# A fused graph layer and two-expert feed-forward: memory of their own for twelve of sixteen slots of unit rows, and rows asked for five units ahead

## The chip, the cores and the metric

One core of one Trainium2 chip runs the kernel. The metric is the device time of one execution in microseconds (us), the median of several runs; lower is better.

## The reference

The input `x` is 128 graphs x 128 nodes x 128 features, so 16,384 tokens. A graph layer is followed by a mixture of eight experts, of which each token uses two.

```python
def reference(x, adj, ...):
    x = x + gnn(layernorm(x), adj, adj, ...)      # two adjacency products per graph, sigmoid gates, relu
    x = x + ffn(layernorm(x), Wg, bg, W1, b1, W2, b2)
    return x

def ffn(xf, ...):                                 # xf: 16384 x 128
    gate_logits = xf @ Wg + bg                    # 8 experts
    top_w, top_i = top_k(gate_logits, 2); top_w = softmax(top_w)
    w_dense = sum(one_hot(top_i, 8) * top_w[..., None], axis=1)
    for e in range(8):                            # W1[e]: 128 x 512, W2[e]: 512 x 128
        out += w_dense[:, e:e+1] * (gelu(xf @ W1[e] + b1[e]) @ W2[e] + b2[e])
    return out
```

How many tokens an expert gets depends on the data; the kernel finds it out as it runs.

## The kernel before, in words

**First phase: 16 chunks.** A chunk is 8 graphs (1,024 tokens). For each chunk the engines work out the graph layer, the second layer norm and the two experts of each token, and write one row of 260 floats per token into `row`, a ring of five chunk slots in the on-chip memory: 128 normed values, 128 values of the running sum, two weights, the row's place in pass two, and the token's number. GpSimd (POOL) then scatters the rows of the chunk into a table `rows` in device memory, eight indirect DMAs of 128 rows per chunk (line 591), sorted by the token's lower expert, in the order of chunks within an expert.

**Second phase: 140 units.** A unit is 256 rows of one expert. Pass one (units 0 to 69) goes through the rows by lower expert, pass two (units 70 to 139) by higher expert; in each pass a few units are blank because experts do not fill their last unit. Per unit:
- SyncE (SP) loads its 256 rows (260 KB) from `rows` into one of `GR` = 16 slots (`rows_in`, line 474), and its biases.
- TensorE (PE) turns the rows (`unit_turned`, line 1377), does layer one (`layer1`, 12 matmuls, lines 1391 to 1393), layer two of the unit before (`layer2`, 12 matmuls, lines 1403 to 1408) and turns the result back (`unit_back`, line 1419). Its program is in order: `layer1(k)`, `unit_back(k-2)`, `layer2(k-1)`, `unit_turned(k+3)`.
- ScalarE does gelu, VectorE splits the hidden values into a high and a low part, weights the result and adds it to the row (`sum_up`).
- POOL scatters the unit's rows: in pass one back into `rows`, to their place in pass two (line 637); in pass two to the output (line 634).

**Weights.** Three slots hold the weights of a layer, so when the expert changes, the next three units each load both layers anew (512 KB a layer, line 490, `layer_in`); otherwise SP just counts the slot's semaphore up. A slot may be overwritten only after the unit three before has read it: layer one's load of unit k+2 waits for the first layer of unit k-1.

**SP's order.** At step k: layer one's weights and the biases of unit k+2, layer two's weights of unit k+1, then the rows of unit k+`AHEAD`, with `AHEAD` = 4. Before step 0 it reads some entries of a unit table that VectorE has worked out, and issues the first `AHEAD` row copies. Everything that SP waits for holds back all that stands behind it.

**Where rows may be loaded, and when.** All sixteen slots of unit rows lie in chunk slots 1 to 4 of the ring `row`: units 0 to 3 in slot 1, which chunk 11 held, units 4 to 7 in slot 2 (chunk 12), 8 to 11 in slot 3 (chunk 13), 12 to 15 in slot 4 (chunk 14). A slot is free once its chunk has been scattered. Also, a unit's rows must have landed in `rows`. `wait_landed` (line 509) sees to both. The first 12 chunks (`PART`) are waited for at the outset. The table gives each of units 0 to 7 a number `least`: 1 if all of its rows come from the first 12 chunks, 5 if it must wait for chunks 12 to 15 as well; POOL counts `s_land` up as each late chunk lands (line 619). Unit 4 waits for `s_land` 2, so that chunk 12 has left slot 2; unit 8 waits for 5, that is for all. In pass two, units 70 to 81 wait for a number of landed units of pass one from the table (`needs`), and unit 82 for all.

Of the kernel before, what the change touches and what calls it, by code (L numbers as in the profile page):

```python
# [8 lines left out]
I32 = mybir.dt.int32  # L9
U32 = mybir.dt.uint32  # L10
ALU = mybir.AluOpType
# [3 lines left out]
P = 128  # L15
G = 8
# [4 lines left out]
BLK = TILE // P  # L21


ROW = 2 * P + 4
W_AT, NEXT_AT, TOKEN_AT = 2 * P, 2 * P + 2, 2 * P + 3
# [3 lines left out]
BIG = float(1 << 23)  # L29
# [24 lines left out]
def wait_turn(eng, sem, each, turn, more):  # L54

    value = turn.group * (each * turn.unroll) + (each * turn.step + more)
    if not isinstance(value, int) or value > 0:
        eng.wait_ge(sem, value)


def wait_slot(eng, sems, each, turn, more):

    ring = len(sems)
    s = turn.slot(ring)
    wait_turn(eng, sems[s], each, Turn(turn.group, (turn.step - s) // ring, turn.unroll // ring, 0), more)
# [20 lines left out]
def program(nc, x, x_turned, adj, edges, gate_weights, gate_biases, Wg, bg, W1, W2, biases, out):  # L86
# [11 lines left out]
    NROWS = 2 * (E - 1) * TOKENS + 2 * TILE  # L98
    UA, UT = 4, 16

    WR, BR, GR, AHEAD = 3, 8, 16, 4

    EARLY = [2 * AHEAD, 3 * AHEAD]

    IN, BACK = 3, 2

# [2 lines left out]
    PART = CHUNKS - 4  # L109

    RING = 5
# [15 lines left out]
    def bank_of_outputs(k):  # L127
        return 5 + 2 * (k + BACK) % 3

    def bank_of_rows(k):  # L130
        return 5 + (2 * (k - IN) + 1) % 3

    w_dram = nc.dram_tensor("w_split", (E, 2, P, 2 * H), F32).ap()
    rows = nc.dram_tensor("rows", (NROWS, ROW), F32).ap()
    out_rows = out.rearrange("b n d -> (b n) d")

    with ExitStack() as ctx:
        def sb(name, shape, dt=F32):
            return ctx.enter_context(nc.sbuf_tensor(name, list(shape), dt))

        def sem(name):
            return ctx.enter_context(nc.semaphore(name))
# [3 lines left out]
        ident = sb("ident", [P, P])  # L146
# [33 lines left out]
        row = sb("row", [P, RING, G, ROW])  # L180
# [55 lines left out]
        skip = sb("skip", [P, UNITS, BLK])  # L236
# [9 lines left out]
        b_t = sb("b_t", [P, BR, FC + 1])  # L246


        assert GR * BLK == 4 * G and (PART - 1) % RING == 1 and GR == 4 * AHEAD
        got = row[:, 1:5].rearrange("p r (s j) k -> p (r s) j k", j=BLK)  # L250
        got_i = got.bitcast(I32)
        to_row = sb("to_row", [P, GR, BLK], I32)
        in_hi = sb("in_hi", [P, IN, TILE], F32R)
        in_lo = sb("in_lo", [P, IN, TILE], F32R)
# [37 lines left out]
        def ps_o(t):  # L292
            return bank[:, bank_of_outputs(t.index), 0:TILE].rearrange("p (j m) -> p j m", j=BLK)

        def ps_x(t):
            return bank[:, bank_of_rows(t.index), 0:TILE]
# [41 lines left out]
        s_land = sem("late_chunks_landed")  # L338
# [38 lines left out]
        def _(sp):  # L377
# [77 lines left out]
            def entries(column, first, n, most, least=0):  # L455
                _, values = nc.values_load_multi_w_load_instructions(
                    table[column:column + 1, bass.ds(first, n)], engines=[mybir.EngineType.SP], min_val=least, max_val=most,
                    skip_runtime_bounds_check_because="VectorE makes the table's entries from counts that lie in these bounds")
                return values
# [9 lines left out]
            def rows_in(t, both):  # L469
                if t.real:  # L470
                    at = sp.snap(both >> 4, min_val=0, max_val=BLANK + 1)
                    g = t.slot(GR)
                    wait_slot(sp, s_out, 16 * BLK, t, 0)
                    sp.dma_start(got[:, g].rearrange("p j k -> p (j k)"),
                                 rows[bass.ds(at, TILE)].rearrange("(p j) k -> p (j k)", j=BLK)).then_inc(s_got[g], 16)

            def layer_in(t, code_, layer):
# [26 lines left out]
            early = entries(PASSES, 0, AHEAD, MOST)  # L504
            least = entries(2 * PASSES + 1, 0, EARLY[0], CHUNKS - PART + 1, 1)
            for i in range(4):
                sp.wait_ge(s_row[i], 16 * G * PART // 4)

            def wait_landed(k, needs):

                if k < EARLY[0]:
                    if k == AHEAD:
                        sp.wait_ge(s_land, 2)
                    sp.wait_ge(s_land, least[k] & 7)
                elif k == EARLY[0]:
                    sp.wait_ge(s_land, CHUNKS - PART + 1)
                if NU <= k < NU + EARLY[1]:
                    sp.wait_ge(s_landed, needs[k - NU] & 127)
                elif k == NU + EARLY[1]:
                    sp.wait_ge(s_landed, NU + 1)  # L520

            for k in range(AHEAD):
                wait_landed(k, None)
                rows_in(unit(k), early[k])
# [6 lines left out]
            for first in range(0, UNITS, UT):  # L531
                if first > 0:
                    now = codes(first, UT + 2)
                if first <= NU - AHEAD < first + UT:
                    early = entries(PASSES + 1, 0, AHEAD, MOST)
                if first < NU + EARLY[1] - AHEAD and first + UT > NU - AHEAD:
                    needs = entries(2 * PASSES, 0, EARLY[1], NU + 1, 1)
                for k in range(first, min(first + UT, UNITS)):
                    i = k - first
                    if k + 2 < UNITS:  # L540
                        layer_in(unit(k + 2), now[i + 2], 0)
                        biases_in(unit(k + 2), now[i + 2])
                    if k + 1 < UNITS:
                        layer_in(unit(k + 1), now[i + 1], 1)
                    if k + AHEAD < UNITS:
                        wait_landed(k + AHEAD, needs)
                        rows_in(unit(k + AHEAD), early[k + AHEAD - NU] if 0 <= k + AHEAD - NU < AHEAD else now[i])
# [4 lines left out]
        def _(pool):  # L552
# [68 lines left out]
            def landed(t):  # L621
                wait_slot(pool, s_out, 16 * BLK, t, 16 * BLK)
                pool.sem_inc(s_landed, 1)

            def scatter(t):
                second = t.index >= NU
                if 0 <= t.index - 3 < NU:
                    landed(t.back(3))
                wait_turn(pool, s_done, 1, t, 1)
                g = t.slot(GR)  # L630
                for j in range(BLK):
                    at = bass.IndirectOffsetOnAxis(ap=to_row[:, g, j:j + 1], axis=0)
                    if second:
                        pool.indirect_dma_start(out=out_rows, out_offset=at, in_=got[:, g, j, P:2 * P], in_offset=None,  # L634
                                                bounds_check=TOKENS - 1, oob_is_err=False).then_inc(s_out[g], 16)
                    else:
                        pool.indirect_dma_start(out=rows, out_offset=at, in_=got[:, g, j, :], in_offset=None,  # L637
                                                bounds_check=NROWS - 1, oob_is_err=False).then_inc(s_out[g], 16)

            for k in range(UNITS):  # L640
                scatter(unit(k))
# [136 lines left out]
        def _(dve):  # L778
# [382 lines left out]
            for i in range(2):  # L1161
# [3 lines left out]
            first, rows_of, seg, lim, at, start = (unit_at_[:, i] for i in range(6))  # L1165
# [7 lines left out]
                                         in1=start_f[:].unsqueeze(1).to_broadcast([P, 2, PASSES]), op0=ALU.mult, op1=ALU.add))  # L1173
# [14 lines left out]
                                         op0=ALU.add, op1=ALU.is_gt))  # L1188
# [21 lines left out]
            for j in range(BLK):  # L1210
                own(dve.scalar_tensor_tensor(out=skips[:, j], in0=ps_ends[:, 0, :, 0:NU], scalar=slot_f[:, j:j + 1],
                                             in1=skips[:, j], op0=ALU.is_gt, op1=ALU.max))
# [17 lines left out]
            def sum_up(t):  # L1230
                g, second = t.slot(GR), int(t.index >= NU)
                wait_turn(dve, s_o, 1, t, 1)
                at = TOKEN_AT if second else NEXT_AT

                dve.scalar_tensor_tensor(out=to_row[:, g, :], in0=skip[:, t.index, :], scalar=BIG, in1=got_i[:, g, :, at],
                                         op0=ALU.mult, op1=ALU.max)
                for j in range(BLK):
                    w = got[:, g, j, W_AT + second:W_AT + second + 1]
                    last = dve.scalar_tensor_tensor(out=got[:, g, j, P:2 * P], in0=ps_o(t)[:, j, :], scalar=w,  # L1239
                                                    in1=got[:, g, j, P:2 * P], op0=ALU.mult, op1=ALU.add)  # L1240
                last.then_inc(s_done, 1)

            units = range(UNITS)
# [9 lines left out]
            for k in units[-BACK - 1:]:  # L1253
                sum_up(unit(k))

        @block.tensor
        def _(pe):
# [108 lines left out]
            for i in range(2):  # L1366
                for k in range(PASSES):
                    last = pe.matmul(ps_ends[:, i, k], ends_rep[:, i, k], ident[:], start=True, stop=True)
            last.then_inc(s_ends_ps, 1)

            def unit_turned(t):
                g = t.slot(GR)
                wait_slot(pe, s_got, 16, t, 16)

                wait_turn(pe, s_done, 1, t, -IN - BACK)
                for j in range(BLK):
                    last = pe.transpose(ps_x(t)[:, j * P:(j + 1) * P], got[:, g, j, 0:P], ident[:])  # L1377
                last.then_inc(s_xt, 1)

            def layer1(t):  # L1380
# [102 lines left out]
```

## Time and profile before

| | |
|---|---|
| runs | 740.89, 740.40, 737.95 us; median 740.4 |
| profiled execution, span from the first to the last instruction | 738.4 us (its time beyond the span is not given) |
| PE busy | 657.4 us, 89% of the span |
| VectorE (DVE) | 617.8 us, 84% |
| ScalarE (ACT) | 525.4 us, 71% |
| POOL | 500.8 us, 68% |
| bytes moved by DMA | 148.47 MB, 201 GB/s over the span |
| mean granted TensorE clock | 0.950 |

In the profile the first phase takes up the first 240 us or so and the units the rest. A wait is put down to the instruction that ended it. The granted clock is a share of full speed (2.4 GHz). The ends of matmuls are modelled, so that PE can be shown busy over a short wait; the weight loads (PEld), which run beside the matmuls, show such waits as well.

### The profile page before, as it was taken

The page shows a single profiled execution, that of the slowest core. Times are in us where ns is not written, and L with a number is a line of the kernel's source. Part 1 is how long each engine was busy: PE and PEld are TensorE (multiplying, and loading weights), DVE is VectorE, ACT ScalarE, POOL GpSimd, SP SyncE. Part 2 cuts the span into 40 slices and gives each one's busy share as a digit, 9 for nine tenths or more (in the row PEclk, how much of TensorE's full clock was granted, in tenths as well). Part 3 has the DMA queues.
Part 4 walks back from the last instruction along what each step waited for, and adds up shares of the span by engine and source line. Part 5 has one row for each costly group of instructions (what it writes and reads, how often), then busy time and mean ns, then how long its engine had stood idle before and what let it go on. Part 6 is the DMA issues. An engine that isn't in the chain of part 4 may idle for free.

```text
span 738.4 us, 17622 instructions
## 1 busy us (share of the span) xinstructions
PE 657.4 (89%) x4878; PEld 598.6 (81%) x4878; DVE 617.8 (84%) x2056; ACT 525.4 (71%) x1470; POOL 500.8 (68%) x469
## 2 busy tenths in 40 slices
PE   6879888998873979999998999999999999999990
PEld 4646666666562879888998999998999999999990
DVE  4899999999997658777887888887888888888881
ACT  5689999999961646666666767766767767767760
POOL 2652767767767857675776776777777777777773
PEclk9999999899955889999999999999999999999996
DMA  8999994547223567599569655499764444444310
GB/s 296 348 369 275 352 324 152 195 147 313 95 87 109 184 175 249 196 339 320 166 213 356 189 163 156 138 325 378 226 168 120 131 122 121 131 124 119 102 40 29
DMA packets 82040, 148.47 MB, mean 201 GB/s; under 512 B 32247, under 2 KB 36352, under 8 KB 81936
## 3 DMA queue, kind: packets, MB, share of 16 engines
q1 hardware_dynamic: 62576, 100.37, 44.3%
q0 software_dynamic: 18496, 46.70, 17.5%
q8 instruction: 41, 0.67, 0.4%
q14 instruction: 63, 0.52, 0.2%
q10 hardware_dynamic: 864, 0.21, 0.1%
HBM read 92.37 MB, written 57.23 MB: 203 GB/s over the span
## 4 chain that ended last, share of the span: by engine, by line
PE 58%; ACT 18%; DMA 8%; DVE 6%; issue 4%; POOL 3%; SPq 1%; POOLq 0%; ACTq 0%; DVEq 0%
PE bank L1391 8%; PE bank L1403 8%; PE bank L1392 8%; PE bank L1393 8%; PE bank L1408 8%; PE bank L1404 8%; DMA row<-rows 7%; ACT hs L687 5%; ACT row L696 5%; PE bank L1377 4%; ACT t_loop L678 4%; PE bank L1419 4%; ACT t_in L671 3%; POOL rows L591 2%; PE bank L1277 1%
## 5 line engine op out<-in xcount | busy, mean ns | idle before, releaser
L756 ACT ACTIVATE act_f<-bank,b_t 128x256 f32<-128x256 f32 x560 | 220.0, 476 | 7.8 <-PE bank L1393 1.6
L637 POOL DMA_INDIRECT rows<-row,to_row x140 | 167.2, 1194 | 74.0 <-issue 51.9
L634 POOL DMA_INDIRECT out_dram<-row,to_row x140 | 168.0, 1200 | 60.2 <-issue 56.4
L591 POOL DMA_INDIRECT rows<-row,slot_low x128 | 136.4, 1066 | 64.5 <-issue 34.8
L1228 DVE TENSOR_TENSOR act_lo<-act_f,act_hi 128x1024 fp32r<-128x1024 f32 x140 | 171.6, 1225 | 4.8
L746 ACT ACTIVATE in_hi<-bank 128x256 fp32r<-128x256 f32 x140 | 53.9, 385 | 154.9 <-PE bank L1377 154.9
L1223 DVE CAST act_hi<-act_f 128x1024 fp32r<-128x1024 f32 x140 | 97.8, 699 | 69.8 <-ACT act_f L756 69.6
L1391 PE MATMUL bank<-in_hi,w_t 128*128 128x256 f32 x376 | 113.5, 302 | 0.0
L1392 PE MATMUL bank<-in_lo,w_t 128*128 128x256 f32 x376 | 105.5, 281 | 0.0
L1393 PE MATMUL bank<-in_hi,w_t 128*128 128x256 f32 x376 | 105.5, 281 | 0.0
L1403 PE MATMUL bank<-act_hi,w_t 128*128 128x256 f32 x376 | 101.2, 303 | 0.2 <-DVE act_hi L1223 0.2
L1404 PE MATMUL bank<-act_hi,w_t 128*128 128x256 f32 x376 | 92.8, 281 | 0.0
L1239 DVE SCALAR_TENSOR_TENSOR row<-bank,row 128x128 f32<-128x128 f32 x280 | 83.7, 338 | 0.0
L1403 PEld LDWEIGHTS bank<-act_hi,w_t 128*128 128x128 f32 x376 | 71.4, 190 | 0.4 <-issue 0.4
L1392 PEld LDWEIGHTS bank<-in_lo,w_t 128*128 128x128 f32 x376 | 71.5, 190 | 0.0
L1404 PEld LDWEIGHTS bank<-act_hi,w_t 128*128 128x128 f32 x376 | 71.5, 190 | 0.0
L1391 PEld LDWEIGHTS bank<-in_hi,w_t 128*128 128x128 f32 x376 | 71.3, 190 | 0.0
L1393 PEld LDWEIGHTS bank<-in_hi,w_t 128*128 128x128 f32 x376 | 71.1, 189 | 0.0
L1377 PE MATMUL bank<-ident,row 128*128 128x128 f32 x280 | 55.8, 281 | 17.2 <-DMA row<-rows 16.6
L763 ACT ACTIVATE y_t<-bank,b_t 128x256 f32<-128x256 f32 x140 | 66.0, 471 | 3.9 <-PE bank L1408 3.9
L1218 DVE TENSOR_TENSOR in_lo<-bank,in_hi 128x256 fp32r<-128x256 f32 x140 | 57.2, 409 | 8.7 <-ACT in_hi L746 8.7
L687 ACT ACTIVATE hs<-xs,shift,rstd 128x128 f32<-128x128 f32 x128 | 53.6, 655 | 8.5 <-DVE t_sum L894 6.7
(225 smaller groups left out, 1658.9 us busy)
## 6 DMA issues: line engine op xcount, KB each, us to landing
row<-rows SPq DMA_DIRECT2D x140, 260.0 KB, 3.7
w_t<-w_split SPq DMA_DIRECT2D x38, 512.0 KB, 6.7
w_up<-w_split SPq DMA_DIRECT2D x18, 512.0 KB, 7.0
xs<-in_x_dram SPq DMA_DIRECT2D x16, 512.0 KB, 5.0
x_t<-in_x_turned_dram SPq DMA_DIRECT2D x16, 512.0 KB, 6.2
rows<-ends_rep SPq DMA_DIRECT2D x15, 260.0 KB, 7.8
b_t<-in_biases_dram SPq DMA_DIRECT2D x140, 2.5 KB
rows<-row,to_row POOLq DMA_INDIRECT x140, 3.7
```

The source lines that it names most:

```text
L591: pool.indirect_dma_start(out=rows, out_offset=bass.IndirectOffsetOnAxis(ap=slot_low[:, r, b:b + 1], axis=0), in_=row[:, r, b, :], in_offs ...
L634: pool.indirect_dma_start(out=out_rows, out_offset=at, in_=got[:, g, j, P:2 * P], in_offset=None, bounds_check=TOKENS - 1, oob_is_err=Fals ...
L637: pool.indirect_dma_start(out=rows, out_offset=at, in_=got[:, g, j, :], in_offset=None, bounds_check=NROWS - 1, oob_is_err=False).then_inc ...
L687: last = act.activation(hs[:, t.slot(2), b, :], xs[:, t.slot(4), b, :], ACT.Identity, scale=rstd[:, 0, b:b + 1], bias=shift[:, 0, b:b + 1])
L756: last = act.activation(act_f[:, s, c, :], ps_h(t, half)[:, i, :], ACT.Gelu, bias=b_t[:, w, c:c + 1])
L1223: dve.tensor_copy(act_hi[:, t.slot(LATE + 1)], act_f[:, t.slot(2)]).then_inc(s_hhi, 1)
L1228: dve.tensor_tensor(act_lo[:, s], act_f[:, t.slot(2)], act_hi[:, s].bitcast(F32), ALU.subtract).then_inc(s_hlo, 1)
L1391: pe.matmul(dst, hi, in_hi[:, s], start=True, stop=False)
L1392: pe.matmul(dst, hi, in_lo[:, s], start=False, stop=False)
L1393: last = pe.matmul(dst, lo, in_hi[:, s], start=False, stop=True)
L1403: pe.matmul(ps_y(t), hi, act_hi[:, s, c, :], start=(c == 0), stop=False)
L1404: pe.matmul(ps_y(t), lo, act_hi[:, s, c, :], start=False, stop=False)
```

## The change

`AHEAD` goes from 4 to 5: SP issues the rows of unit k+5 at step k, and five row copies before step 0. Twelve of the sixteen slots of unit rows get a buffer of their own, `own_rows`; the other four lie in ring slot 1, which chunk 11 held. With that the wait of unit 4 for `s_land` 2 falls away, units 0 to 11 wait by the table's `least`, and unit 12 waits for all. In pass two, units 70 to 82 go by `needs` and unit 83 waits for all.

```diff
-    WR, BR, GR, AHEAD = 3, 8, 16, 4
-
-    EARLY = [2 * AHEAD, 3 * AHEAD]
+    WR, BR, GR, AHEAD = 3, 8, 16, 5
+    OWN_ROWS = 12
+
+    EARLY = [OWN_ROWS, 13]
...
-        assert GR * BLK == 4 * G and (PART - 1) % RING == 1 and GR == 4 * AHEAD
-        got = row[:, 1:5].rearrange("p r (s j) k -> p (r s) j k", j=BLK)
-        got_i = got.bitcast(I32)
+        assert (PART - 1) % RING == 1 and (GR - OWN_ROWS) * BLK == G
+        own_rows = sb("own_rows", [P, OWN_ROWS, BLK, ROW])
+        left_rows = row[:, 1].rearrange("p (s j) k -> p s j k", j=BLK)
+        got = [own_rows[:, g] for g in range(OWN_ROWS)] + [left_rows[:, g] for g in range(GR - OWN_ROWS)]
+        got_i = [held.bitcast(I32) for held in got]
...
             def wait_landed(k, needs):
                 if k < EARLY[0]:
-                    if k == AHEAD:
-                        sp.wait_ge(s_land, 2)
                     sp.wait_ge(s_land, least[k] & 7)
                 elif k == EARLY[0]:
                     sp.wait_ge(s_land, CHUNKS - PART + 1)
```

The other edits write `got[g]` for `got[:, g]`. The counts of table entries that SP reads follow from `AHEAD` and `EARLY`: at the start 5 + 12 instead of 4 + 8, at the start of pass two 5 + 13 instead of 4 + 12.

## Rows read from the trace of the kernel before

**Rows 1.** The page's costliest groups: busy us, mean ns, then idle before, releaser.
```profile
L1377 PE MATMUL bank<-ident,row 128*128 128x128 f32 x280 | 55.8, 281 | 17.2 <-DMA row<-rows 16.6
```
**Rows 2.** Waits in 286-300, 300-345, 380-405, 485-525: us in total, times, longest.
```profile
PEld bank L1377 <- DMA row<-rows: 2.7, 2, 1.9
...
PEld bank L1377 <- DMA row<-rows: 4.0, 5, 1.7
...
PEld bank L1377 <- DMA row<-rows: 2.8, 4, 1.1
...
PEld bank L1377 <- DMA row<-rows: 3.2, 9, 1.0
```
**Rows 3.** The chain of waits, 264-715: start us, us, what.
```profile
275.63 0.47 PE bank L1408 x4
278.89 0.48 PE bank L1408 x4
...
290.05 8.12 DMA row<-rows
```
**Rows 4.** Windows: stretch, length, PE, PEld, DVE, ACT, POOL busy, PEclk, DMA share, GB/s.
```profile
264.00:269.50 5.50, 5.50 (x29) 5.50 (x29) 1.85 (x3) 2.43 (x6) 4.28 (x5) 0.56 0.90 239
...
325.00:335.00 10.00, 7.99 (x67) 7.59 (x66) 7.22 (x17) 5.53 (x15) 6.33 (x6) 1.00 1.03 407
...
500.00:520.00 20.00, 19.70 (x162) 18.70 (x162) 15.14 (x34) 13.60 (x36) 13.96 (x12) 1.00 1.04 378
```
**Rows 5.** Timeline of SP's DMA issues in stretch A: start us, us, line, copy.
```profile
289.32 0.33 SPq L490 DMA_DIRECT2D w_t<-w_split  x1
290.05 0.33 SPq L474 DMA_DIRECT2D row<-rows  x1
```
**Rows 6.** The same, three weight loads of stretches B, C and D.
```profile
331.60 0.33 SPq L490 DMA_DIRECT2D w_up<-w_split  x1
...
389.20 0.33 SPq L490 DMA_DIRECT2D w_t<-w_split  x1
...
511.82 0.33 SPq L490 DMA_DIRECT2D w_t<-w_split  x1
```
**Rows 7.** Line 490 alone: landings of the copies of 289.32, 331.60, 389.20, 511.82.
```profile
DMA to landing us min/median/max: 7.7/7.7/7.7
...
DMA to landing us min/median/max: 7.5/7.5/7.5
...
DMA to landing us min/median/max: 8.2/8.2/8.2
...
DMA to landing us min/median/max: 6.5/6.5/6.5
```
**Rows 8.** PE's timeline: the first matmuls that read these four weight copies.
```profile
300.02 0.36 PE L1403 MATMUL bank<-act_hi,w_t 128*128 128x256 f32 x1
...
341.62 0.36 PE L1391 MATMUL bank<-in_hi,w_up 128*128 128x256 f32 x1
...
399.77 0.36 PE L1391 MATMUL bank<-in_hi,w_t 128*128 128x256 f32 x1
...
520.54 0.37 PE L1391 MATMUL bank<-in_hi,w_t 128*128 128x256 f32 x1
```
**Rows 9.** Unit 7: SP's issues, PE's transposes (idle before in brackets), SP's own waits.
```profile
261.16 0.33 SPq L474 DMA_DIRECT2D row<-rows  x1
262.11 0.34 SPq L502 DMA_DIRECT2D b_t<-in_biases_dram  x1
...
263.81 0.69 PE L1377 MATMUL bank<-ident,row 128*128 128x128 f32 x2 [4.69 <-DMA row<-rows]
...
SPq L474 <- POOLq L619: 9.7, 1, 9.7
```
**Rows 10.** SP's first issues of the unit phase.
```profile
237.67 2.21 SPq L474 DMA_DIRECT2D row<-rows  x4
242.79 2.41 SPq L502 DMA_DIRECT2D b_t<-in_biases_dram  x3
```

More of the change, by code:

```diff
@@ L473, in rows_in @@
                     wait_slot(sp, s_out, 16 * BLK, t, 0)
-                    sp.dma_start(got[:, g].rearrange("p j k -> p (j k)"),
+                    sp.dma_start(got[g].rearrange("p j k -> p (j k)"),
                                  rows[bass.ds(at, TILE)].rearrange("(p j) k -> p (j k)", j=BLK)).then_inc(s_got[g], 16)
@@ L633, in scatter @@
                     if second:
-                        pool.indirect_dma_start(out=out_rows, out_offset=at, in_=got[:, g, j, P:2 * P], in_offset=None,
+                        pool.indirect_dma_start(out=out_rows, out_offset=at, in_=got[g][:, j, P:2 * P], in_offset=None,
                                                 bounds_check=TOKENS - 1, oob_is_err=False).then_inc(s_out[g], 16)
                     else:
-                        pool.indirect_dma_start(out=rows, out_offset=at, in_=got[:, g, j, :], in_offset=None,
+                        pool.indirect_dma_start(out=rows, out_offset=at, in_=got[g][:, j, :], in_offset=None,
                                                 bounds_check=NROWS - 1, oob_is_err=False).then_inc(s_out[g], 16)
@@ L1233, in sum_up @@
                 at = TOKEN_AT if second else NEXT_AT
-                dve.scalar_tensor_tensor(out=to_row[:, g, :], in0=skip[:, t.index, :], scalar=BIG, in1=got_i[:, g, :, at],
+                dve.scalar_tensor_tensor(out=to_row[:, g, :], in0=skip[:, t.index, :], scalar=BIG, in1=got_i[g][:, :, at],
                                          op0=ALU.mult, op1=ALU.max)
                 for j in range(BLK):
-                    w = got[:, g, j, W_AT + second:W_AT + second + 1]
-                    last = dve.scalar_tensor_tensor(out=got[:, g, j, P:2 * P], in0=ps_o(t)[:, j, :], scalar=w,
-                                                    in1=got[:, g, j, P:2 * P], op0=ALU.mult, op1=ALU.add)
+                    w = got[g][:, j, W_AT + second:W_AT + second + 1]
+                    last = dve.scalar_tensor_tensor(out=got[g][:, j, P:2 * P], in0=ps_o(t)[:, j, :], scalar=w,
+                                                    in1=got[g][:, j, P:2 * P], op0=ALU.mult, op1=ALU.add)
                 last.then_inc(s_done, 1)
@@ L1376, in unit_turned @@
                 for j in range(BLK):
-                    last = pe.transpose(ps_x(t)[:, j * P:(j + 1) * P], got[:, g, j, 0:P], ident[:])
+                    last = pe.transpose(ps_x(t)[:, j * P:(j + 1) * P], got[g][:, j, 0:P], ident[:])
                 last.then_inc(s_xt, 1)
```

## The prediction

> **What bounds the kernel now.** I read the page's costliest groups first, then the waits, the chain, stretches of the window view, and the SP and PE timelines.
>
> In the unit phase (about 240 to 728 us) TensorE sets the pace. The chain advances one unit in 278.89 - 275.63 = 3.26 us [rows 3]. At the first matmul of a layer PE is never idle; the only PE group with real idle time ahead of it is the transpose of a unit's rows, 17.2 us, 16.6 of it for `row<-rows` copies [rows 1]. So the question is where those waits lie and what ends them. By the weight-load side of the waits view, which also sees the short ones, they lie in four stretches, in each of which SP fetches new weights: A (286 to 300) 2.7 us, B (300 to 345) 4.0, C (380 to 405) 2.8, D (485 to 525) 3.2, together 12.7 us, no single wait above 1.9 [rows 2]. The rest of the unit phase shows none. A fifth wait, 4.69 us before 263.81, is another matter: SP itself waited 9.7 us there for POOL's word that the late chunks had landed [rows 9]. The clock stays at 1.00 through B and D, short waits included; only behind the 4.69 us wait is it 0.56 (1.2 GHz for most of that stretch, else 2.4) [rows 4].
>
> Why rows come late in a stretch: SP issues in order, at step k first layer 0's weights of unit k+2 (held until the first layer of unit k-1 is done), the bias, layer 1's weights of unit k+1, then the rows of unit k+4. In A a weight copy issued at 289.32 stands right ahead of the row copy issued at 290.05 [rows 5], which takes 8.12 us to land [rows 3]. PE wants the rows at the end of step k+1, about two and a half steps (8 us) after SP was let go.
>
> **Rows asked five units ahead.** Each row copy moves one place forward: unit u's copy stands where unit u-1's stands now, behind the same weights. No copy is added and the order of sizes in the queue is the same. That buys 3.26 us of lead [rows 3] against single waits of at most 1.9 [rows 2], and it holds as long as less than 3.26 us is regained in a stretch. All 12.7 us are then no longer rows' fault.
>
> What is late next: the weights. PE runs earlier by what it regains, so the weight copies must have that much slack. The load nearest to late in each stretch:
> - A: layer 1 of unit 13, issued 289.32 + 7.7 = 297.0 [rows 5, 7], used 300.02 [rows 8]: 3.0 us spare against 2.7 lost. All 2.7 come back.
> - B: layer 0 of unit 26, 331.60 + 7.5 = 339.1 [rows 6, 7], used 341.62 [rows 8]: 2.5 spare against 4.0. 2.5 come back.
> - C: layer 0 of unit 43, 389.20 + 8.2 = 397.4 [rows 6, 7], used 399.77 [rows 8]: 2.4 against 2.8. 2.4 come back.
> - D: layer 0 of unit 79, 511.82 + 6.5 = 518.3 [rows 6, 7], used 520.54 [rows 8]: 2.2 against 3.2. 2.2 come back.
>
> Sum 9.8 us, if the weights land exactly when they do now. They may land earlier, since many are held until PE's matmuls are done and those come earlier: the upper bound is all 12.7. They may land later, since the scatters of finished units also come up to 2.5 us earlier and push bytes ahead of them: at most 2.5/3.26 of a unit's 266 KB (256 rows of 260 floats), 0.2 MB, at the 407 GB/s of B [rows 4] 0.5 us in each of B, C and D, lower bound 8.3. I take 10.4, near the fixed landings, because the DMA share of 1.03 and 1.04 in B and D [rows 4] leaves little room for earlier ones.
>
> A rule is weighed here. The rows show 407 GB/s at most, at a share of 1.03 [rows 4]. The Trainium skill, "DMA: Bandwidth & Descriptors", section Specifications, puts the fabric's ceiling at 435 GB/s. By it a step with two 512 KB loads, 260 KB of rows and a scatter as large (1.58 MB) would need 3.63 us (an estimate), 0.37 more than the pitch; over the 25 units that load weights 9.3 of the 12.7 us would stay and the time would be 737.0. No run here shows that ceiling; 407 is below it and agrees. The mechanism is a rival below.
>
> **Own memory for twelve slots, and the wait dropped for the fifth unit's rows.** The copies of units 4 to 11 no longer need chunk 12, 13 or 14 out of the row memory, and unit 4 no longer waits for two late chunks. Neither was what ended last: SP came through its first seven row copies without a wait, and its one wait on POOL is the 9.7 us [rows 9]. I cost this at nothing, either way.
>
> **First twelve units wait only for what they read.** In the kernel before, units 0 to 7 already wait by the table entry `least`. The eighth row copy (unit 7) is the one issued at 261.16, after that wait [rows 9]. So its entry already says "all late chunks", and it will say so again. The first weight load for another expert belongs to unit 12, so units 8 to 11 are later rows of the same expert and their entries say the same. The 4.69 us wait and the slow clock behind it stay. What changes is the place: SP now meets this wait one step earlier, with layer 0's mark of unit 5, bias 5 and layer 1's mark of unit 4 still behind it in its queue. PE does not miss them: its in-order program stops at unit 7's transpose, ahead of all three. After the release SP put the next bias out at 262.11 [rows 9], 0.95 us behind the rows; PE restarts at 263.81 and gelu of unit 5 needs six matmuls more. Cost 0. Without that cover it is the bias's landing, which no row gives; the nearest is the 1.7 us from its issue to PE's restart, which is spare now. Below nothing: POOL's late scatters could end sooner if units start later, and a shorter idle could spare the slow clock; at most 5.5 x (1 - 0.56) = 2.4 us [rows 4]. I take 0.
>
> **The start.** SP reads five more table entries and issues a fifth row copy ahead of the first bias. Four copies took 2.21 us, 0.62 a copy from start to start, and from their end to the first bias 242.79 - 239.88 = 2.9 us pass for eighteen entries and more [rows 10], so at most 0.16 an entry: 0.62 + 5 x 0.16 = 1.4 us at most, at least 0. PE's first unit comes that much later, and the 4.69 us wait for POOL swallows it, since POOL's scatters do not wait for PE. Cost 0; 1.4 if that wait were gone.
>
> **The pass boundary.** Unit 78's rows are asked one step earlier and need every unit of pass one landed. SP showed no wait on POOL but the 9.7 us [rows 9], so I take 0; at worst one step, 3.26 us, once.
>
> **Sum.** Profiled span 738.4 - 10.4 = 728.0 us. The page gives no more than the span; the runs' median 740.4 lies 2.0 above it, the lowest, 737.95, just below, so what lies around the span can't be told from the scatter of runs. I carry the 2.0 along: 730.0.
>
> **Rivals.**
> - *The stretches are bound by bytes.* At a share of 1.03 the queue is full [rows 4], asking sooner only makes copies wait longer, and scatters brought forward delay the weights as much as PE gains. Then B and D give back nothing, A and C 2.7 + 2.4 = 5.1: 735.3. Against it: every weight in B and D still has 2.2 us or more to spare [rows 6 to 8], and the bytes in a stretch do not grow. Chance 0.13.
> - *The dropped wait does what its words say*: units 7 to 11 go on without the late chunks, the 4.69 us and up to 2.4 us of slow clock go too, less 1.4 at the start: 730.0 - 5.7 = 724.3. Only if the table's entry for unit 7 is not what SP waited on. Chance 0.03.
> - *Slower: the waits merge and the clock falls.* The short row waits become one wait for weights in each stretch. Idles up to 1.9 us left the clock at 1.00, one of 4.69 halved it [rows 2, 4, 9]; it decides when a merged wait passes from the one towards the other. All 12.7 us would stay, and a halved clock costs up to 2.4 us in each of four stretches: 740.4 + 9.6 = 750.0. For it: B's 4.0 us in one piece would be near 4.69. Against: the slack leaves at most 4.0 - 2.5 = 1.5 us to wait for weights. Chance 0.04.
>
> **How the numbers follow.** Forecast 0.77 (its own range 727 to 732.5: gains of 12.7 to 8.3 and a microsecond of scatter), bytes 0.13, dropped wait 0.03, slower 0.04, and 0.03 that something unseen eats the gain. What a measurement of this kernel can tell from no change is about 0.5%, 3.7 us. Faster: the forecast, the dropped wait and two thirds of the bytes case, 0.88; same 0.08; slower 0.04. Range 726.5 to 735.5: it takes in the bounds of the forecast and most of the bytes case.
>
> **What would show it.** PE's transposes wait for `row<-rows` about 0 in A and C and under 2 us in B and D together; new idle appears ahead of the matmuls that read `w_t` and `w_up`, about 1.5 us in B, 0.4 in C, 1.0 in D; the wait of about 4 to 5 us before unit 7's transpose stays, as does SP's wait on POOL; row copies in the stretches still take 6 to 9 us. I am wrong if the row waits stay, if weights land more than a microsecond later than now, or if unit 7 starts with the others.

## The result: 730.26 us against 739.17, and the profile after

The changed kernel takes 730.26 us (median of 4 runs, 729.03 to 732.82), the kernel before 739.17 beside it (4 runs, 737.37 to 740.89). The ratio is 0.9876, 95% interval 0.9841 to 0.991: 9 us faster, against a forecast of 730.0 and a range of 726.5 to 735.5. The profiled execution of the changed kernel has a span of 730.8 us and a time of 732.82, so 2.0 us lie around its span.

The number is right; three of the terms behind it are not, and they cancel in part. Line numbers below are those of the changed kernel: the transpose of the rows is L1379 (before L1377), layer one's first matmul L1393 (L1391), layer two's L1405 (L1403), weight loads L494, row copies L478, the count of a weight slot that needs no load L499 (L495). In the kernels of the experiments they shift by a few lines.

The groups of PE that answer to [rows 1] and the first matmul of layer one (busy us, mean ns, idle before and its releaser):

```profile
L1393 PE MATMUL bank<-in_hi,w_t 128*128 128x256 f32 x376 | 114.3, 304 | 2.3 <-SPq L499 1.5 <-DMA w_t<-w_split 0.8
...
L1393 PE MATMUL bank<-in_hi,w_up 128*128 128x256 f32 x184 | 55.6, 302 | 1.7 <-SPq L499 1.3 <-DMA w_up<-w_split 0.4
...
L1379 PE MATMUL bank<-ident,own_rows 128*128 128x128 f32 x216 | 42.4, 278 | 6.6 <-DMA own_rows<-rows 6.6
```

The transposes' 6.6 us lie at the start (4.59, 0.22, 0.32) and ahead of unit 7 (1.44). In the stretches they wait for nothing; the first matmul of a layer does. The waits of the weight-load side over 264 to 560 us (total us, times, longest), first of the kernel before, then after:

```profile
PEld bank L1377 <- DMA row<-rows: 12.8, 20, 1.9
```

```profile
PEld bank L1393 <- SPq L499: 3.4, 3, 1.7
PEld bank L1393 <- DMA w_t<-w_split: 1.7, 4, 0.8
PEld bank L1393 <- DMA w_up<-w_split: 0.7, 1, 0.7
PEld bank L1405 <- SPq L499: 0.4, 2, 0.2
```

"SPq L499" is to be read with care. At that line SP counts a weight slot's semaphore up for a unit that needs no new load, once the slot's last load has landed, so its mark follows the landing at once. In stretch A the weights of unit 14 were issued at 283.87 and took 8.7 us, which is 292.57; PE's matmul started at 292.60. The wait is one for weights, whichever name it has (SP's issue, its landing, PE's matmul with its idle in brackets):

```profile
283.87 0.33 SPq L494 DMA_DIRECT2D w_up<-w_split  x1
...
DMA to landing us min/median/max: 8.7/8.7/8.7
...
292.60 0.38 PE L1393 MATMUL bank<-in_hi,w_up 128*128 128x256 f32 x1 [0.52 <-SPq L499]
```

So 12.8 us of waits for rows (12.7 in the four stretches of [rows 2]) became 6.2 us of waits for weights: 0.8 in A, 2.2 in B, 2.3 in C, 1.0 in D.

The two loads that the prediction held nearest to late in B and C, layer 0 of units 26 and 43, in the changed kernel:

```profile
323.94 0.33 SPq L494 DMA_DIRECT2D w_up<-w_split  x1
...
DMA to landing us min/median/max: 10.0/10.0/10.0
...
334.00 0.39 PE L1393 MATMUL bank<-in_hi,w_up 128*128 128x256 f32 x1 [0.74 <-SPq L499]
...
382.02 0.33 SPq L494 DMA_DIRECT2D w_t<-w_split  x1
...
392.15 0.39 PE L1393 MATMUL bank<-in_hi,w_t 128*128 128x256 f32 x1 [1.46 <-SPq L499]
```

The first took 10.0 us to land instead of 7.5 [rows 7]. For the second the view gives no landing; PE got it 10.1 us after its issue, where it had landed in 8.2 before.

Around unit 7, to be held against [rows 9] and the stretch behind it in [rows 4] (SP's issue, PE's transpose, SP's wait, then the window of 264 to 269.5 with the clock third from the end):

```profile
259.53 0.33 SPq L478 DMA_DIRECT2D own_rows<-rows  x1
...
262.16 0.44 PE L1379 MATMUL bank<-ident,own_rows 128*128 128x128 f32 x2 [1.44 <-DMA own_rows<-rows]
...
SPq L478 <- POOLq L621: 9.8, 1, 9.8
...
264.00:269.50 5.50, 5.50 (x50) 5.50 (x48) 4.22 (x8) 3.63 (x11) 4.05 (x5) 1.00 0.84 244
```

SP waits for POOL as long as before, so unit 7's entry does say "all late chunks". But PE idles 1.44 us instead of 4.69, and the clock stays up. Units reached this point 1.6 us later (transpose of unit 6 at 257.28 instead of 255.71), and POOL was through earlier: unit 7's rows were issued at 259.53 instead of 261.16.

Last, the step, that is the time from one unit to the next on PE, over 32 units in which nothing waits: the transposes of units 100 and 132, first of the kernel before, then after.

```profile
582.34 0.38 PE L1377 MATMUL bank<-ident,row 128*128 128x128 f32 x2
...
686.52 0.38 PE L1377 MATMUL bank<-ident,row 128*128 128x128 f32 x2
```

```profile
573.92 0.38 PE L1379 MATMUL bank<-ident,own_rows 128*128 128x128 f32 x2
...
678.76 0.38 PE L1379 MATMUL bank<-ident,own_rows 128*128 128x128 f32 x2
```

104.18 / 32 = 3.256 us before, 104.84 / 32 = 3.276 after. The 28 matmuls and transposes of a unit start 117.0 ns apart on the mean instead of 116.3. Over 130 units that is 2.7 us lost, in a place where no wait shows.

The two spans, 738.4 and 730.8, balance like this, by the transposes' starts: everything up to unit 10 -3.9 us (start and wait ahead of unit 7), the four stretches -6.4 (what their steps take over the undisturbed step went from 13.4 to 7.0), the longer step +2.7.

### The profile page after: what moved, and what is told of

Read it like the earlier page. It is cut to its first block and busy times, and to the rows that moved or that the text cites. A ratio compares the mean times of both kernels' runs of the same rounds, so it can differ in the third digit from the quotient of the medians.

```text
span 730.8 us, 17628 instructions
## 1 busy us (share of the span) xinstructions
PE 657.9 (90%) x4878; PEld 600.2 (82%) x4878; DVE 619.9 (85%) x2056; ACT 524.6 (72%) x1470; POOL 500.9 (69%) x469
## 2 busy tenths in 40 slices
DMA packets 82039, 148.45 MB, mean 203 GB/s; under 512 B 32247, under 2 KB 36352, under 8 KB 81936
## 5 line engine op out<-in xcount | busy, mean ns | idle before, releaser
L639 POOL DMA_INDIRECT rows<-own_rows,to_row x108 | 129.3, 1197 | 53.1 <-issue 40.2
L636 POOL DMA_INDIRECT out_dram<-own_rows,to_row x108 | 128.7, 1192 | 46.8 <-issue 43.0
L1393 PE MATMUL bank<-in_hi,w_t 128*128 128x256 f32 x376 | 114.3, 304 | 2.3 <-SPq L499 1.5
L1405 PE MATMUL bank<-act_hi,w_t 128*128 128x256 f32 x376 | 100.9, 302 | 0.1
L1393 PEld LDWEIGHTS bank<-in_hi,w_t 128*128 128x128 f32 x376 | 71.9, 191 | 3.7 <-SPq L499 1.7
L1405 PEld LDWEIGHTS bank<-act_hi,w_t 128*128 128x128 f32 x376 | 70.9, 189 | 0.7 <-SPq L499 0.4
L1241 DVE SCALAR_TENSOR_TENSOR own_rows<-bank,own_rows 128x128 f32<-128x128 f32 x216 | 64.6, 339 | 0.0
L1410 PE MATMUL bank<-act_lo,w_t 128*128 128x256 f32 x376 | 59.8, 281 | 0.0
```

Of the source, the lines that this page charges most:

```text
L639: pool.indirect_dma_start(out=rows, out_offset=at, in_=got[g][:, j, :], in_offset=None, bounds_check=NROWS - 1, oob_is_err=False).then_inc ...
L1393: pe.matmul(dst, hi, in_hi[:, s], start=True, stop=False)
L1405: pe.matmul(ps_y(t), hi, act_hi[:, s, c, :], start=(c == 0), stop=False)
L1410: last = pe.matmul(ps_y(t), hi, act_lo[:, s, c, :], start=False, stop=(c == FC - 1))
```

## Experiments

Theory after the result: the gain is the fifth unit of lead in the four stretches, cut short by weights that land late; own memory gives nothing and costs the longer step. Rival: a good part of the gain comes from the start (own memory, the wait ahead of unit 7).

**e1 and e2: both kernels once more, unchanged.**

> The changed kernel once more. In its first profile PE's step from unit to unit was 3.28 us late in the run (before: 3.26), TensorE's clock did not fall after the wait ahead of unit 7, and that wait was 1.4 us long (before: 4.69). If these belong to the change, all three come again: step 3.28, wait 1 to 2 us, clock 1.00. If they belong to the single execution, at least the step goes back to 3.26 and the span lies near 727 to 728. Either way the row waits in the four stretches stay gone and PE waits for weights there.

> The kernel before once more: row waits of about 12 to 13 us in the four stretches. If the wait of 4.69 us ahead of unit 7 and the fallen clock behind it belong to the kernel, both come again and the step is 3.26 us; if they are one execution's, the wait is 3 us or less or the clock stays.

e1: 732.58 us (4 runs), ratio to the kernel before 0.9879 (0.9823 to 0.9934). Step 3.276 again, the step from unit 6 to unit 7 1.8 us longer than the others, clock 1.00, 6.9 us of waits for weights. e2: one run, 742.46 us, step 3.256. But its wait ahead of unit 7 was short and the clock did not fall behind it:

```profile
263.36 0.44 PE L1377 MATMUL bank<-ident,row 128*128 128x128 f32 x2 [1.66 <-DMA row<-rows]
...
264.00:269.50 5.50, 5.50 (x50) 5.50 (x49) 3.33 (x7) 4.46 (x12) 3.97 (x4) 1.00 0.86 236
```

The step belongs to the kernel. The 4.69 us wait and the slow clock do not come in every execution of the kernel before: in e2 the units started 2 us later, and PE met a shorter wait. So the first pair of profiles does not show that the change won those 4 us. How often either length comes, two profiles can't say. The stretches of e2 cost more than in the first profile, 16.1 us of row waits against 12.8:

```profile
PEld bank L1377 <- DMA row<-rows: 16.1, 19, 2.3
```

And in e2 the clock fell inside a stretch, which it did not do in the first profile (PE's wait in C, then the window behind it):

```profile
399.28 0.44 PE L1377 MATMUL bank<-ident,row 128*128 128x128 f32 x2 [1.97 <-DMA row<-rows]
...
399.90:403.30 3.40, 3.40 (x18) 3.40 (x17) 0.70 (x2) 2.28 (x6) 1.94 (x2) 0.50 0.61 183
```

PE had idled 1.05 us at 393.84 and 1.97 us here, and the next 3.4 us ran at half clock (1.2 GHz), which costs at most 1.7 us (an estimate, half of 3.4). In e3 below the same follows an idle of 2.19 us in A: 0.50 from 295.8 to 299.2.

**e3 and e4: the two halves of the change alone.** e3 takes the changed kernel with

```diff
-    WR, BR, GR, AHEAD = 3, 8, 16, 5
+    WR, BR, GR, AHEAD = 3, 8, 16, 4
...
-    EARLY = [OWN_ROWS, 13]
+    EARLY = [OWN_ROWS, 12]
```

and e4 the kernel before with

```diff
-    WR, BR, GR, AHEAD = 3, 8, 16, 4
-    EARLY = [2 * AHEAD, 3 * AHEAD]
+    WR, BR, GR, AHEAD = 3, 8, 16, 5
+    EARLY = [8, 13]
...
-                    if k == AHEAD:
+                    if k == 4:
                         sp.wait_ge(s_land, 2)
```

> Own memory and the dropped waits, with rows asked four units ahead as before. Theory (the gain is the fifth unit of lead in the four stretches): ratio 0.99 to 1.00 to the kernel before, 735 to 739 us, row waits of 11 to 13 us in the stretches. Rival (the gain is at the start: own memory, units 4 to 11 and the wait ahead of unit 7): 730 to 733 us with the row waits still there.

> Rows asked five units ahead with the memory of the kernel before (unit 4 still waits for two late chunks, units 8 and on for all). Theory: the whole gain, 729 to 732 us, row waits below 1 us in the stretches. Rival (own memory and the start): 736 to 740 us.

e3: 740.33 us (10 runs, a little above the 735 to 739 expected), ratio 1.0009 (0.9977 to 1.004), nothing gained; its row waits are all there (weight-load side, 264 to 560):

```profile
PEld bank L1379 <- DMA own_rows<-rows: 10.1, 11, 2.4
PEld bank L1379 <- DMA row<-rows: 2.9, 7, 0.8
```

e4: 729.03 us (4 runs), ratio 0.9853 (0.9796 to 0.9909), the whole gain. No wait for rows is left in the stretches. What is left is 3.9 us for weights:

```profile
PEld bank L1391 <- DMA w_t<-w_split: 1.9, 3, 1.2
PEld bank L1391 <- SPq L495: 1.4, 2, 1.0
PEld bank L1391 <- DMA w_up<-w_split: 0.4, 1, 0.4
PEld bank L1403 <- SPq L495: 0.2, 1, 0.2
```

Theory holds, the rival falls. The steps are 3.276 in e3, 3.256 in e4: the longer step comes with `own_rows`, not with the lead. e3 should by that be 2.7 us slower than before; its interval reaches 3 us, so the times neither show nor exclude it.

**e5 and e6: what makes the step longer.** e5 is the changed kernel with `own_rows` allocated last, e6 is e4 with a dead tensor:

```diff
-        own_rows = sb("own_rows", [P, OWN_ROWS, BLK, ROW])
         to_row = sb("to_row", [P, GR, BLK], I32)
...
         y_t = sb("y_t", [P, BACK, TILE])
+        own_rows = sb("own_rows", [P, OWN_ROWS, BLK, ROW])
```

```diff
+        dead = sb("dead", [P, 12, BLK, ROW])
         to_row = sb("to_row", [P, GR, BLK], I32)
```

> The changed kernel with own_rows allocated behind all other on-chip tensors, so that in_hi, in_lo, act_hi, act_lo and the rest lie where they lay before. PE's step was 3.276 us in every profile with own_rows ahead of them and 3.256 in every one without. Theory (it is where these tensors lie): step 3.256, 140 x 0.02 = 2.9 us less than the changed kernel, 728 to 730 us. Rival (it is that rows are read from and written to own_rows): step 3.276, 731 to 733 us.

> Rows five ahead with the memory of before, and an unused tensor of the size of own_rows (24,960 bytes a partition) where own_rows stood. Nothing reads or writes it. Theory (where the tensors lie): step 3.276 us. Rival (use of own_rows): step 3.256.

e5: 728.36 us (4 runs), ratio 0.9856 (0.9837 to 0.9874). Units 100 and 132 of e5, then of e6 (one run, 730.72 us):

```profile
570.50 0.38 PE L1379 MATMUL bank<-ident,own_rows 128*128 128x128 f32 x2
...
674.74 0.38 PE L1379 MATMUL bank<-ident,own_rows 128*128 128x128 f32 x2
```

```profile
572.16 0.38 PE L1378 MATMUL bank<-ident,row 128*128 128x128 f32 x2
...
676.93 0.38 PE L1378 MATMUL bank<-ident,row 128*128 128x128 f32 x2
```

104.24 / 32 = 3.257 and 104.77 / 32 = 3.274. A tensor that nobody touches makes the step longer, and one that is used does not if it lies behind the others. So it is where the tensors allocated behind it lie, among them the operands that the matmuls stream in. Which of them, and which offsets are good, was not tried. By the times the 2.7 us do not show: e9 below is e5 once more, and the changed kernel's ratios of 0.9876 and 0.9879 lie between e5's 0.9856 and e9's 0.989.

**e7: half of the weight bytes.** e5 without the loads of layer two's weights when the expert changes (SP only counts the slot up), by this in `layer_in`:

```diff
+                    if layer == 1:
+                        wait_slot(sp, sems, 16, t, 0)
+                        sp.sem_inc(sems[k], 16)
+                        return
                     with sp.If_ne(sp.to_reg(held), 8):
```

> Rows five ahead, own_rows last, and layer two's weights never loaded anew (the output is wrong for it): half of the weight bytes are gone. Theory (what is left of the waits in the four stretches is weights that land late because the DMA queues are full): all waits in the stretches go, span 721 to 724. Rival (the waits come from SP's order or from something else in a change of expert): 3 to 6 us of them stay, span 725 to 728.

One run, 724.37 us, span 721.4. PE has no wait left between 264 and 560 us, and the steps of all four stretches are 3.257. What is left of the waits is weight loads and nothing else; but halving bytes also shortens each landing, so this alone does not say whether bytes or the moment of the request decide. e10 does.

**e8: rows eight units ahead.** e5 with `AHEAD` 8 and `EARLY = [OWN_ROWS, 16]`.

> Own_rows last, rows eight units ahead. Theory (behind the fifth unit the weights are late, no longer the rows): no gain over five ahead, 728 to 731 us, with the same waits for weights in B, C and D; the start may cost some tenths. Rival (rows are still what counts): 724 to 727 us.

748.32 us (4 runs), ratio 1.0119 (1.0091 to 1.0146): slower, and my expectation missed by far. SP's first eight issues of the phase (start, time from first to last), PE's idle, and SP's two waits on POOL, for the late chunks (L621) and at the pass boundary (L625):

```profile
245.31 19.34 SPq L478 DMA_DIRECT2D own_rows<-rows  x8
...
266.54 0.58 PE L1393 MATMUL bank<-in_hi,w_t 128*128 128x256 f32 x1 [12.87 <-SPq L499]
...
SPq L478 <- POOLq L621: 14.7, 1, 14.7
...
SPq L478 <- POOLq L625: 7.1, 1, 7.1
```

The eighth copy is unit 7's, which waits 14.7 us for POOL. With eight ahead it stands before SP's first step, so the marks that let PE begin layer one of unit 0 queue behind it: PE idles 12.87 us. The wait that the forecast costed at nothing with five ahead, because PE's own program stops first, costs this once it stands three steps further forward. The pass boundary does the same (7.1 us on POOL's count of landed units), and the steps of D lose 6.4 us instead of 2.1. In B and C the steps lose 2.3 and 1.1 us as in e5 (2.1 and 0.9): there more lead for rows indeed gives nothing. Some 7 us of the profiled span lie ahead of SP's first row copy (245.31, in e9 237.82), in the first phase, and have no part in this.

**e9 to e12: can it be better?** All on e5; e9 is e5 again, as the measure in the same series (its 730.41 us lie just above the 728 to 730 expected). e10 has a fourth slot for the weights of a layer; e11 waits at the outset for the first 14 chunks instead of 12, and the table's `least` goes by these:

```diff
-    WR, BR, GR, AHEAD = 3, 8, 16, 5
+    WR, BR, GR, AHEAD = 4, 8, 16, 5
...
-        w1_slot = [w1_t[:, 0], w1_t[:, 1], w_up[:, 0]]
-        w2_slot = [w2_t[:, 0], w2_t[:, 1], w_up[:, 1]]
+        w1_slot = [w1_t[:, 0], w1_t[:, 1], w_up[:, 0], w_up[:, 2]]
+        w2_slot = [w2_t[:, 0], w2_t[:, 1], w_up[:, 1], w_up[:, 3]]
```

```diff
-    PART = CHUNKS - 4
+    PART = CHUNKS - 2
...
-                sp.wait_ge(s_row[i], 16 * G * PART // 4)
+                sp.wait_ge(s_row[i], 16 * G * ((PART - i + 3) // 4))
...
             def last_counts(t):
+                if t.index == PART:
+                    dve.tensor_copy(part[:], count[:, :, G]).then_inc(s_part, 1)
+                    dve.wait_ge(s_part, 1)
```

e12 has both.

> Rows five ahead with own_rows last, once more, as the measure for the three kernels beside it: 728 to 730 us, step 3.256 us, waits of 1 to 2 us each in B, C and D, an excess of 1.5 us in the step from unit 6 to unit 7.

> The same with four slots of weights instead of three: a load is let go one unit earlier, but a change of expert loads up to four units anew, some 29 units instead of 25. Theory (the weights land late because the queues are full of bytes): the waits in B, C and D don't go, each more load brings 1 MB, 2.6 us at 407 GB/s, against 3.26 us of lead: within 1.5 us of e9 either way. Rival (it is the moment at which a load is let go): the waits of 4.5 to 5.2 us go, 723 to 725 us.

> The same as e9, with the first 14 chunks waited for at the outset and counted for the table's least instead of the first 12, so that units 7 and 8 need not wait for chunks 14 and 15. Theory (the wait ahead of unit 7 is for rows that land late): the step from unit 6 to 7 is 3.26 us and 1 to 1.7 us are gained over e9, 726.5 to 728. Rival (the start comes later by waiting for chunk 13, or POOL's scatters take longer beside more units): no gain or a loss of up to 2 us.

> Four weight slots and the first 14 chunks together. By the theories of e10 and e11: e11's time within 1.5 us, 725 to 729. By e10's rival: 721 to 724.

| kernel (6 runs each) | us | ratio to the kernel before | 95% interval |
|---|---|---|---|
| e9, e5 again | 730.41 | 0.989 | 0.9859 to 0.9921 |
| e10, four weight slots | 725.46 | 0.982 | 0.9783 to 0.9858 |
| e11, first 14 chunks | 727.92 | 0.9862 | 0.9825 to 0.9899 |
| e12, both | 724.00 | 0.9795 | 0.9763 to 0.9828 |

e10 goes against the theory of my expectation and with its rival. All the waits for weights are gone. The windows of its four stretches (PE and PEld busy first, then DVE, ACT, POOL; clock, DMA share, GB/s last), and the one wait of PEld left between 264 and 560:

```profile
283.00:300.00 17.00, 17.00 (x148) 17.00 (x147) 14.96 (x34) 12.29 (x33) 12.43 (x11) 1.00 1.02 377
315.00:345.00 30.00, 30.00 (x259) 29.89 (x258) 26.20 (x55) 21.36 (x57) 22.35 (x19) 1.00 1.03 390
378.00:400.00 22.00, 22.00 (x192) 22.00 (x191) 19.16 (x42) 15.45 (x42) 16.38 (x14) 1.00 0.98 371
485.00:515.00 30.00, 30.00 (x261) 30.00 (x259) 26.31 (x57) 21.49 (x57) 22.14 (x19) 1.00 1.05 379
```

```profile
PEld bank L1379 <- DMA own_rows<-rows: 0.5, 1, 0.5
```

It moves 5.3 MB more than the changed kernel (153.71 against 148.45) and a load takes 8.6 us on the median to land, against 7.8 in e9, yet PE never waits for one. The landings of all loads, e9 first, then e10:

```profile
DMA to landing us min/median/max: 4.0/7.8/10.2
```

```profile
DMA to landing us min/median/max: 3.4/8.6/11.3
```

So what was late was the request: with three slots a load is let go about 8 us before its use, under the landing times of 8 to 10 us late in a stretch, with four 3.26 us sooner. A DMA share of 1.03 was no sign that PE must wait. The bytes do count in another way: along a stretch loads land later and later, in e10's D from 3.4 us at its head to 10.5, so bytes are asked for faster there than they are moved. Four slots cover this over stretches as long as these; longer ones were not tried. The profiled execution of e10 also began its units 3.7 us later than that of e9 (transpose of unit 0 at 245.28 and 241.57), after 58 us at half clock instead of 44, so its span, 724.6, shows less of the gain than its steps do: 6.0 us over the undisturbed step in e9's stretches, 0.1 in e10's. Whether the fourth slot has a part in the later start is open.

e11: the transposes of units 6 and 7, 3.25 us apart, no wait:

```profile
257.55 0.38 PE L1382 MATMUL bank<-ident,own_rows 128*128 128x128 f32 x2
...
260.80 0.38 PE L1382 MATMUL bank<-ident,own_rows 128*128 128x128 f32 x2
```

In e9 they are 5.03 us apart. The 1.8 us are shown by the profile; by the times e11 and e9 overlap. The intervals of e10 and e9 just fail to meet. e12 is the fastest kernel of the study, about 2% faster than the one before and, by intervals that do not overlap, faster than the changed one.

## Why the prediction was right, point by point

- **Rows asked five ahead: right.** Waits for rows in the stretches went from 12.8 us to 0, and the lead alone gives the whole gain (e4: 0.9853; e3: 1.0009). One premise was too narrow: the stretches cost more than the waits in them where the clock falls behind a wait. It did so after idles of 1.97 us (e2) and 2.19 us (e3) with rows four ahead, and in no stretch of the changed kernel, e1 or e4. The prediction had a falling clock in these stretches only as a rival, for merged waits after the change.
- **"What is late next: the weights": right in kind, mis-sized.** Forecast 0, 1.5, 0.4 and 1.0 us left in A to D; measured 0.8, 2.2, 2.3 and 1.0, so about 6.5 us came back instead of 10.4, below the lower bound of 8.3 too. The step that failed is "if the weights land exactly when they do now", with 0.5 us as the bound on later landings. The load nearest to late landed 2.5 us later in B (10.0 us instead of 7.5), and in C PE got it 10.1 us after its issue instead of a landing in 8.2. That meets one of the prediction's own signs of being wrong, weights that land more than a microsecond later. Why they land later is argued, not tested: when PE no longer waits for rows, its matmuls let the next loads go sooner, and the queue fills faster. Across the kernels with five ahead and three weight slots (e7 and e8 left aside) the waits for weights come to 3.7 to 6.9 us, and the row waits with four ahead to 12.8 (before), 16.1 (e2) and 13.0 (e3): one profile of each was too few to size this term to a microsecond.
- **Own memory "at nothing, either way": wrong.** The moved tensors make each step 0.02 us longer, 2.7 us in all by the profiles (e5, e6). I had bounded waits and looked at no address.
- **"The 4.69 us wait and the slow clock stay": wrong in size, for want of a second profile.** SP's wait on POOL stayed, as argued from unit 7's entry. PE's idle was 1.66 us in a second profile of the kernel before, whose units started later (e2). So the 4 us that the first pair of profiles seems to give here can't be counted as a gain of the change.
- **The start: right.** PE's transpose of unit 0 came 0.6 us later, that of unit 6 1.6, among it 0.8 us by which the first gelu waited longer for its bias behind five row copies (2.0 us against 1.2); the wait for POOL swallowed it. One reading was incomplete: the clock was down not only behind the 4.69 us wait, but also through the first units, at half speed until 245.0 in the kernel before and until 247.8 in the changed one.
- **The pass boundary: right** with five ahead; e8 shows its price.
- **The rival of bytes, and the page's rule.** The rival fell: B and D gave back 1.9 and 2.0 us by their steps, and e10 runs all stretches at 3.257 us with more bytes. The Trainium skill, "DMA: Bandwidth & Descriptors", Specifications, gives 435 GB/s as the fabric's ceiling. The highest window shown here, 407 GB/s [rows 4], lies below it and agrees; no run shows the ceiling itself. The estimate of 3.63 us a step that I made from it does not hold: it counted 1.58 MB a step, 485 GB/s at the step of 3.26, while e10 moves 371 to 390 GB/s over its stretches at that step. Those windows also hold steps without loads, and what the others ask for beyond that rate shows as later landings, not as longer steps.
- **The sum: in part luck.** In the first pair of profiles: stretches -6.4 instead of -10.4, own memory +2.7 instead of 0, the first units with the start -3.9 instead of 0. The first two miss the same way, by 6.7 us together, and the third makes up for 3.9 of it in that pair, so the profiled span was 730.8 against the 728.0 forecast; that execution was the slowest of the four, and their median is 730.26. By the times the lead without the longer step gives ratios of 0.9853 (e4), 0.9856 (e5) and 0.989 (e9, the same kernel as e5), some 8 to 11 us, around the forecast's 10.4. The stretches of the kernel before cost more in some executions than in the one I had read (e2, with a fallen clock).

## What to carry to other kernels

When a wait is taken away, look up how much time the next thing has from request to landing in a full queue, and move its request too: one more weight slot brought as much again as half of the whole change. In an in-order queue a wait that is asked for earlier blocks everything behind it; it is free only as long as its consumer stops first. And after any new buffer compare the undisturbed step of the busiest engine to the nanosecond, since a moved tensor shows in no wait.

## What the hardware showed unexpectedly

PE's step between undisturbed units depends on where the on-chip tensors lie: 3.256 or 3.257 us in the ten profiles without 24,960 bytes a partition ahead of `to_row` and the tensors behind it (before, e2, e4, e5, e7 to e12), 3.274 to 3.276 in the four with them (after, e1, e3, e6). POOL's indirect scatters of the late chunks took 0.97 us each, with few exceptions, until some microseconds into the units, and several took 1.68 us or more after that: four of the last eight in the kernel before (1.89 us at most), three of the last eight in the changed kernel, whose units began later. That units that start later let POOL finish sooner fits this and was not tested by itself. And 512 KB loads that land in 3.5 us at the head of a stretch mostly take 8 to 10 us late in it with rows five ahead, and some 6 to 9 us with four.
